# Cross attention rewritten: transposed scores of both heads in row halves, one maximum over a pair's columns, division behind the values

## What is computed

```python
B, N, M = 4, 1024, 77          # batches, queries, keys of the context
H, DH = 16, 64                 # heads; two heads make a pair, so 8 pairs a batch
cross_in = _adaln(x, cond, ...)
ctx_n = _ln(context, ca_lnc_w, ca_lnc_b)
q = _heads(cross_in @ wq); k, v = jnp.split(ctx_n @ wkv, 2, axis=-1)
q, k = _rope(q, sq, cq), _rope(_heads(k), sk, ck)
sim = jnp.einsum('bhnd,bhmd->bhnm', q, k) * DH ** (-0.5)
a = jax.nn.softmax(sim, axis=-1)
o = jnp.einsum('bhnm,bhmd->bhnd', a, _heads(v))
x = o.reshape(...) @ wo + bo + x
```

## Time and profile before

| | us |
|---|---|
| median of 3 runs | 2492.4 (2489.9 to 2494.3) |
| profiled execution | 2491.1 |
| its span in the trace | 2489.3 |
| self attention, from its first load to its last store | 68.5 to 1637.8 |
| cross attention, from its first matmul to the next stage's first load | 1735.9 to 2254.2 |

### The profile page before, as it was taken

One profiled execution on the slowest core, in us unless ns is written; L12 is line 12 of the kernel. 1 busy time (PEld: TensorE's weight loads), 2 busy tenths in 40 slices (PEclk: granted clock), 3 DMA queues, 4 the chain that ended last, 5 costly groups with the idle time before them and its releaser, 6 DMA issues. The chain is left out here.

```text
span 2489.3 us, 40040 instructions
## 1 busy us (share of the span) xinstructions
PE 2229.8 (90%) x15036; PEld 1041.0 (42%) x15036; DVE 1865.8 (75%) x2926; ACT 1330.6 (53%) x1655; POOL 352.3 (14%) x199
## 2 busy tenths in 40 slices
PE   2489999999999999999999999955799999994899
PEld 2133333344333334333334333342456566563566
DVE  6568999986898986898996898665675666665553
ACT  5257676664667664667664666534443434344221
POOL 3100000000000000000000000012653636452100
PEclk9589999999999999999999999976898999996999
DMA  4101101011111010101001100052332323224211
GB/s 163 54 26 40 39 30 41 35 44 43 44 35 44 35 41 30 61 35 44 35 27 44 60 36 20 17 168 54 94 102 72 96 76 93 84 84 128 62 42 34
DMA packets 106254, 143.81 MB, mean 58 GB/s; under 512 B 28209, under 2 KB 74367, under 8 KB 106111
## 3 DMA queue, kind: packets, MB, share of 16 engines
q1 hardware_dynamic: 106111, 141.87, 17.8%
HBM read 55.70 MB, written 12.85 MB: 28 GB/s over the span
## 5 line engine op out<-in xcount | busy, mean ns | idle before, releaser
L625 PE MATMUL sa_ps_o<-sa_probs,sa_v_pair 128*64 128x512 f32 x2048 | 533.5, 615 | 2.9 <-DVE sa_mx L845 2.9
L769 ACT ACTIVATE sa_probs<-sa_ps_s 128x1024 f32<-128x1024 f32 x512 | 495.8, 1025 | 26.2 <-PE sa_ps_s L612 26.2
L845 DVE CUSTOM_DVE_ANT_0 sa_rise<-sa_ps_t,sa_rise 128x512 f32<-128x512 f32 x512 | 333.1, 688 | 200.7 <-PE sa_ps_t L591 200.4
L858 DVE TENSOR_TENSOR sa_acc<-sa_acc,sa_probs 128x1024 f32<-128x1024 f32 x384 | 462.4, 1246 | 7.2 <-ACT sa_probs L769 7.2
L757 ACT ACTIVATE sa_rise<-sa_ps_t 128x1024 f32<-128x1024 f32 x256 | 261.8, 1023 | 258.8 <-PE sa_ps_t L584 258.8
L561 POOL TENSOR_TENSOR sa_xr<-sa_xr,sa_bo_row 128x1024 f32<-128x1024 f32 x8 | 22.6, 2843 | 1322.7 <-DMA sa_xr<-in_x 1322.7
L625 PEld LDWEIGHTS sa_ps_o<-sa_probs,sa_v_pair 128*64 128x64 f32 x2048 | 102.1, 135 | 247.3 <-issue 174.5
L605 PE MATMUL sa_ps_s<-sa_hi 64*128 64x512 f16 x1024 | 194.5, 376 | 0.0
L605 PE MATMUL sa_ps_s<-sa_hi,sa_lo 64*128 64x512 f16 x1024 | 194.4, 376 | 0.0
L605 PE MATMUL sa_ps_s<-sa_lo,sa_hi 64*128 64x512 f16 x1024 | 194.4, 376 | 0.0
L612 PE MATMUL sa_ps_s<-sa_m_line,sa_m_ones 64*128 64x512 f16 x1024 | 189.5, 377 | 1.3 <-DMA sa_m_line<-sa_m_rows 1.3
(11 more groups left out here) (266 smaller groups left out, 4597.5 us busy)
## 6 DMA issues: line engine op xcount, KB each, us to landing
sa_swp<-sa_raw SPq DMA_DIRECT2D x128, 256.0 KB, 2.4
ca_swp<-ca_raw SPq DMA_DIRECT2D x70, 256.0 KB, 2.4
sa_inv<-sa_scratch SPq DMA_DIRECT2D x128, 128.0 KB, 2.9
ca_q_hl<-ca_hi SPq DMA_DIRECT2D x68, 128.0 KB, 2.3
ca_q_hl<-ca_lo SPq DMA_DIRECT2D x68, 128.0 KB, 2.3
sap_xs<-in_x SPq DMA_DIRECT2D x4, 1024.0 KB, 7.0
sa_xr<-in_x SPq DMA_DIRECT2D x4, 1024.0 KB, 5.8
cap_xs<-x_after_self SPq DMA_DIRECT2D x4, 1024.0 KB, 7.0
```

The lines of the kernel that those rows point to most:

```text
L625: ins = pe.matmul(ps_o[rows(x), half(c)], v_pair[:, kt, rows(x)], probs[:, kt % 2, c, half(x)], start=(kt == 0), stop=(kt == NK - 1))
L769: act.activation(probs[:, kt % 2, c, :], ps_s[c][:, :], ACT.Exp, scale=float(DH) ** -0.5).then_inc(s_p, 1)
L845: dve.tensor_tensor_reduce(out=rise[:, half(x)], in0=turn[x], in1=rise[:, half(x)], scale=1.0, scalar=-3.0e38, op0=ALU.add, op1=ALU.max, a ...
L858: dve.tensor_tensor(acc[:, c, :], before, probs[:, kt % 2, c, :], ALU.add).then_inc(s_acc[c], 1)
```

## The change

In `project_context` the upper and lower parts of the keys are written straight into `k_hi` and `k_lo`, both heads of a pair above one another, and the DMAs that stacked them are gone. `cross_attention` is new from its tiles to its order, which is now unrolled:

- The scores are computed twice. `bases` makes the 16-bit product of the upper parts with queries on the partitions, 16 matmuls of 64 rows (8 blocks x 2 heads), only to find a maximum. `maxima` (DVE) takes it over the 77 keys for each query and head, 128 x 16 numbers in one instruction. PE turns them, ACT makes `m_rows` of them (`row`), SP copies these into `m_line` with 4 DMAs (`line`), and PE adds them with `shift`. `scores` makes the three products with the keys on the partitions, for both heads in the two row halves of the array.
- ACT takes the exponentials from PSUM straight into `probs`, keys on the partitions, so the turning of the weights is gone. `values` multiplies at once.
- The sums come from PE (`totals`). ACT brings them to SBUF, SP gathers them (4 DMAs), DVE inverts them, SP writes them to DRAM, waits, and spreads them (4 DMAs). DVE divides the output behind the values (`normalise`, three instructions for each half), three pairs later.
- The rotation is all on DVE (`turned`), and the `q_hl` copies are gone. POOL only adds the bias.
- The output projections of batches 0 to 2 run inside pairs 10, 18 and 26; the last one runs in two parts.

The core of the diff; lines that went with the old stage are left out:

```diff
@@ -983,14 +980,7 @@
                 sp.dma_start(swp[0:P:2, half(n)], raw[1:P:2, half(n)]).then_inc(s_swap[n], 16)
                 sp.dma_start(swp[1:P:2, half(n)], raw[0:P:2, half(n)]).then_inc(s_swap[n], 16)
             for n in range(2):
-                sp.wait_ge(s_hi, n + 1)
-                for x in range(2):
-                    for dst in (k_hh[0:DH], k_hh[DH:P]):
-                        sp.dma_start(dst[:, half(n), x], hi[DH * x:DH * x + DH, half(n)]).then_inc(s_stack, 16)
-                sp.wait_ge(s_lo, n + 1)
-                for x in range(2):
-                    sp.dma_start(k_lo[:, half(n), x], lo[DH * x:DH * x + DH, half(n)]).then_inc(s_stack, 16)
-            sp.wait_ge(s_stack, 16 * 12)
+                sp.wait_ge(s_swap[n], 32)
...
+            def swap(j):
                 sp.wait_ge(s_q_r, 2 * j + 2)
+                if j >= 2:
+                    sp.wait_ge(s_rot, j - 1)
+                sp.dma_start(swp[0:P:2, j % 2, :], raw[1:P:2, j % 2, :]).then_inc(s_swap[j % 2], 16)
+                sp.dma_start(swp[1:P:2, j % 2, :], raw[0:P:2, j % 2, :]).then_inc(s_swap[j % 2], 16)
+            def line(j):
+                sp.wait_ge(s_mt_r, j + 1)
+                for c in range(2):
+                    for x in range(2):
+                        at = TT * c + TT // 2 * x
+                        sp.dma_start(m_line[DH * x:DH * x + 1, half(c)], m_rows[at:at + TT // 2, :]).then_inc(s_line, 16)
+            def gather_sums(g):
+                sp.wait_ge(s_sum_r, g + 1)
+                if g >= 1:
+                    sp.wait_ge(s_scr, 16 * g)
+                for n in range(4):
+                    sp.dma_start(few[32 * n:32 * n + 32, :], sums[32 * n:32 * n + 1, :]).then_inc(s_few, 16)
+            def spread_inverses(g):
+                sp.wait_ge(s_rec, g + 1)
+                if g >= 1:
+                    sp.wait_ge(s_inv, 64 * g)
+                    sp.wait_ge(s_div, 2 * g)
+                sp.dma_start(scratch.rearrange("n (i k) -> (n i) k", k=16), few[:]).then_inc(s_scr, 16)
+                sp.wait_ge(s_scr, 16 * (g + 1))
+                for c in range(2):
+                    for x in range(2):
+                        sp.dma_start(inv[rows(x), half(c)],
+                                     scratch[2 * c + x].partition_broadcast(DH)).then_inc(s_inv, 16)
...
+            for g in range(G + 3):
+                if g == G:
+                    gather_sums(G - 2)
+                if g == G + 1:
+                    gather_sums(G - 1)
+                if 2 <= g < G:
+                    gather_sums(g - 2)
+                if g + 2 < G:
+                    swap(g + 2)
+                if g < G:
+                    line(g)
+                if 2 <= g < G + 2:
+                    spread_inverses(g - 2)
+                if output_batch(g) is not None:
+                    b = output_batch(g)
+                    sp.wait_ge(s_yr, TT * (b + 1))
+                    sp.dma_start(y_v[b], xr[:]).then_inc(s_out, 16)
+                    sp.wait_ge(s_out, 16 * (b + 1))
+                    sp.dma_start(xr[:], x_v[b + 1]).then_inc(s_x, 16)
...
+            def bases(g):
+                b, pair = g // PAIRS, g % PAIRS
                 for t in range(TT):
+                    c, at = t // 4, t % 4 * M
+                    for x in range(2):
+                        ins = pe.matmul(ps_s[:, c, x * HALF + at:x * HALF + at + M],
+                                        hi[rows(x), g % 3, t * P:(t + 1) * P], k_hi[rows(x), pair, b, :],
+                                        start=True, stop=True)
+                ins.then_inc(s_base, 1)
+            def scores(g):
+                b, pair, s = g // PAIRS, g % PAIRS, g % 3
+                for c in range(2):
+                    for n, (k, q) in enumerate(((k_hi, hi), (k_lo, hi), (k_hi, lo))):
+                        for x in range(2):
+                            pe.matmul(ps_s[0:M, c, half(x)], k[rows(x), pair, b, :], q[rows(x), s, half(c)],
+                                      start=(n == 0), stop=False)
+            def shift(g):
+                for c in range(2):
+                    for x in range(2):
+                        ins = pe.matmul(ps_s[0:M, c, half(x)], m_ones[rows(x), 0:M], m_line[rows(x), half(c)],
+                                        start=False, stop=True)
+                    ins.then_inc(s_st, 1)
...
+            def totals(g):
+                for c in range(2):
+                    for x in range(2):
+                        n = 2 * c + x
+                        ins = pe.matmul(turn[0][32 * n:32 * n + 32, :], ones32[0:M, 0:32], probs[:, g % 2, c, half(x)],
+                                        start=True, stop=True)
+                ins.then_inc(s_sum, 1)
...
+            for g in range(G):
+                pe.wait_ge(s_hi, g + 1)
+                if g >= 1:
+                    pe.wait_ge(s_p, 2 * g)
+                bases(g)
+                if g + 3 < G:
+                    if g == 0:
+                        pe.wait_ge(s_q_r, 2 * 2 + 1)
+                    if g >= 2:
+                        pe.wait_ge(s_sum_r, g - 1)
+                    if output_batch(g - 1) is not None:
+                        pe.wait_ge(s_yr, TT * (output_batch(g - 1) + 1))
+                    project(g + 3, 0)
+                pe.wait_ge(s_max, g + 1)
+                pe.wait_ge(s_q_r, 2 * min(g + 3, G))
+                if output_batch(g - 1) is not None:
+                    pe.wait_ge(s_yr, TT * (output_batch(g - 1) + 1))
+                pe.transpose(turn[1][0:2 * TT, 0:P], mx[:, g % 2, :], ident[:, :]).then_inc(s_mt, 1)
+                pe.wait_ge(s_lo, g + 1)
+                scores(g)
+                if g >= 1:
+                    values(g - 1)
+                pe.wait_ge(s_line, 64 * (g + 1))
+                shift(g)
+                if g >= 1:
+                    if g + 3 < G:
+                        pe.wait_ge(s_q_r, 2 * (g + 3) + 1)
+                    elif g >= 2:
+                        pe.wait_ge(s_sum_r, g - 1)
+                    totals(g - 1)
+                if g + 3 < G:
+                    pe.wait_ge(s_mt_r, g + 1)
+                    project(g + 3, 1)
...
+            def evacuate_q(j, c):
+                act.wait_ge(s_q, 2 * j + c + 1)
+                if j >= 2:
+                    act.wait_ge(s_lo, j - 1)
+                act.activation(raw[:, j % 2, half(c)], turn[c], ACT.Copy, scale=1.0 / WS).then_inc(s_q_r, 1)
...
+            def row(g):
+                act.wait_ge(s_mt, g + 1)
+                act.activation(m_rows[:], turn[1][0:2 * TT, 0:P], ACT.Copy, scale=-1.0 / MS).then_inc(s_mt_r, 1)
...
+            for g in range(G):
+                if g + 3 < G:
+                    evacuate_q(g + 3, 0)
+                row(g)
+                if g >= 1:
+                    evacuate_o(g - 1, 0)
+                for c in range(2):
+                    exponentials(g, c)
+                if g >= 1:
+                    evacuate_o(g - 1, 1)
+                    evacuate_sums(g - 1)
+                if g + 3 < G:
+                    evacuate_q(g + 3, 1)
+                if g + 2 < G:
+                    high(g + 2)
+            evacuate_o(G - 1, 0)
+            evacuate_o(G - 1, 1)
...
+            def turned(j):
+                dve.wait_ge(s_swap[j % 2], 32 * (j // 2 + 1))
+                dve.tensor_tensor(raw[:, j % 2, :], raw[:, j % 2, :], ropeC[:, :], ALU.mult).then_inc(s_mul, 1)
+                dve.tensor_tensor(swp[:, j % 2, :], swp[:, j % 2, :], ropeS[:, :], ALU.mult).then_inc(s_mul, 1)
+                dve.wait_ge(s_mul, 2 * (j + 1))
+                dve.tensor_tensor(raw[:, j % 2, :], raw[:, j % 2, :], swp[:, j % 2, :], ALU.add).then_inc(s_rot, 1)
+            def low(j):
                 dve.wait_ge(s_hi, j + 1)
+                dve.tensor_tensor(lo[:, j % 3, :], raw[:, j % 2, :], hi[:, j % 3, :], ALU.subtract).then_inc(s_lo, 1)
+            def maxima(g):
+                dve.wait_ge(s_base, g + 1)
+                banks = ps_s.rearrange("p c (x n) -> p (c x) n", x=2)[:, :, 0:4 * M]
+                dve.reduce_max(mx[:, g % 2, :], banks.rearrange("p a (t m) -> p a t m", m=M), AX_X).then_inc(s_max, 1)
+            def reciprocals(g):
+                dve.wait_ge(s_few, 64 * (g + 1))
+                dve.reciprocal(few[:], few[:]).then_inc(s_rec, 1)
+            def normalise(g, c):
+                n, cs = 2 * g + c + 1, half(c)
+                dve.wait_ge(s_inv, 64 * (g + 1))
+                dve.wait_ge(s_oev, n)
+                dve.tensor_tensor(o_pair[:, g % 2, cs], o_pair[:, g % 2, cs], inv[:, cs], ALU.mult).then_inc(s_div, 1)
+                dve.wait_ge(s_div, n)
+                dve.tensor_copy(o_hi[:, g % PAIRS, cs], o_pair[:, g % 2, cs]).then_inc(s_ohi, 1)
+                dve.wait_ge(s_ohi, n)
+                dve.tensor_tensor(o_lo[:, g % PAIRS, cs], o_pair[:, g % 2, cs], o_hi[:, g % PAIRS, cs],
+                                  ALU.subtract).then_inc(s_ot, 1)
...
```

(85 more changed lines are left out.)

373 lines of the change are left out of this document (114 added, 259 removed).

## The result

| | before | after |
|---|---|---|
| median, us | 2493.4 (2489.9 to 2498.6, 4 runs) | 2597.8 (2596.9 to 2600.9, 4 runs) |
| span of the profiled execution, us | 2489.3 | 2599.1 |
| PE busy in the span | 90% | 85% |

The profiled execution took 2600.9 us, where the prediction had 2602.

What follows compares the result with a forecast made beforehand. PE bounds the old kernel; in the new one the chain through DVE, ACT, SP and PE does. Stage 55 + 445 + 66 + 22 + 48 = 636 us against 518.3, less 6.5 for its earlier start: 2603 us, range 2545 to 2655.

Steps and rivals of the forecast that it cites:

- the chain: One pair's waits through PE, DVE, ACT and SP: 12.4 us before the last step, 17.1 with it, against 12.0 before.
- Row and line: From ACT's start on the row to the first matmul on the line, with four SP DMAs: 4.2 us.
- The last step: PE's shift, totals and half a projection: 2.95 us at the upper clock, 5.4 after idling; taken as 4.7.
- Two lists: Work per pair on two queues: SP issuing 15 DMAs, 9.6 us; DVE's instructions, 10.3 us; both staying behind the chain.
- Rival 1: PE's clock holds in the last step: pair 15.4 us, stage 591, kernel 2558 us; chance 0.22.
- three output projections: Output projections inside pairs lie open, since DVE and ACT run through their lists and wait: 3 x 22 = 66 us.
- pairs 29 and 30: Late pairs where no evacuation stands ahead of the row: 11 us each, 22 us.
- end: After the last maxima: outputs of pairs 29 to 31 divided in turn, then last projection part and store: 48 us.
- SP's delay behind an output: After each output projection SP waits for the store, gathers and swaps before the line: about 1 us late.
- Rival 2: Narrow matmuls are slow and keep the clock down: bases 2.2 us, pair 19.4, kernel about 2663 us; chance 0.13.
- Rival 3: The chain isn't closed; ACT goes straight to the row: pair 10.5 us, kernel 2431, deciding point 12.8; chance 0.07.
- Rival 4: Row halves don't run side by side with 77 key columns: shift 0.43 us more per pair, kernel 2614 us; chance 0.03.

Runs made afterwards that it cites:

- low_first: Changed kernel with one edit on DVE: low(g+1) directly behind maxima(g), ahead of normalise(g-3). 2495.8 us.
- row_first: Changed kernel with one edit on ACT: the row of maxima of pair g ahead of the query copy for pair g+3. 2482.6 us.
- fill: Changed kernel with the scores of each pair computed three times more, where PE waits for the line. 2564.5 us.
- line2: Changed kernel with the line of maxima copied by two DMAs of eight rows instead of four. 2563.7 us.
- row_low_line: Changed kernel with row ahead of the copy on ACT, low(g+1) ahead of normalise(g-3) on DVE, and the line in two DMAs. 2456.9 us.
- row_low_line_fill: row_low_line with the scores of each pair computed once more than needed, behind the values. 2443.7 us.
- fill4: Changed kernel with the scores of each pair computed four times more, where PE waits for the line. 2563.8 us.

## Why the prediction was right, point by point

**The bound and the chain.** PE does not set the pair; the chain over DVE, ACT and SP does. PE's own work fell from 81.78 us in seven pairs, 11.7 each at a granted clock of 0.93, to 8.4 at 1.00 (the first row of `low_first` above), and the pair still grew. `low_first` and `row_first` each break it at one link and give back 102 and 115 us, where the whole loss was 104. Here the pair by its steps, predicted and measured in the timeline above:

| step | predicted | measured |
|---|---|---|
| first of `bases` to DVE's start on `maxima` | 1.25 | 0.75 |
| `maxima` | 1.43 | 1.44 |
| to the start of `low` (division of g-3) | 3.65 | 3.49 |
| `low`, to ACT's start on the copy | 1.25 | 1.31 |
| copy | 0.65 | 0.49 |
| row, line, to `shift` (1877.52 to 1881.44) | 4.2 | 3.92 |
| `shift`, `totals`, projection | 4.7 | 5.54 |
| pair | 17.1 | 16.94 |

The mechanism is right. Three terms were mis-sized, and that they cancelled to within 0.2 us was luck. `bases` were put 0.5 us too long: the 64-row matmuls that alternate between row halves take 0.70 us for 16, 0.044 each, below both bounds of the prediction (0.056 and 0.14). Row and line were put 0.3 us too long. The last step was put 0.8 us too short: taken at 4.7 between 2.95 and 5.4, it is 5.54 in the trace, above the upper end that the earlier trace rows gave. That end had the clock come back after 4.9 us. Here all matmuls of the step ran at the lower clock, and the first at the upper one (0.38 us) starts at 1888.82, 7.4 us behind the shift. Two lists were put too long without a part in the sum: SP issues for 9.0 us a pair, not 9.6, and DVE has 9.7 us and not 10.3. DVE's 9.7 became the bound of the short pairs above. That DVE doesn't wait for the inverses holds at 17 us, but no longer at 14.

**The clock.** The prediction took the lower clock for most of the step because of an idle time of 6.2 us; it was 5.42. The page "TensorE: Matmul & The Clock Gate" of the Trainium skill, section "HAM oscillation — how this bites in real kernels", has a loop that waits for a DMA in every tile start each one cold. With that the trace agrees: the seven pairs ahead of the first output projection stand at a granted clock of 0.70 and last 16.9 to 17.0 us. Rival 1, the upper clock throughout, is what `fill` brought about in part, with a last step of 2.95 us and pairs of 14.1.

**The line.** The prediction added 1.4 us to the 2.8 of two DMAs. It was 1.1: 2.78 in `line2`, 3.92 here. What it gave for two DMAs less, 36 us, `line2` measured at 34; 26 x 1.14 are 30 of them, the rest came from the clock.

**The stage.** In us:

| part | predicted | measured |
|---|---|---|
| start, to `bases` of pair 3 | 55 | 54.5 |
| 26 pairs | 445 | 440.4 |
| three output projections | 66 | 70.4 |
| pairs 29 and 30 | 22 | 19.4 |
| end | 48 | 49.3 |
| stage | 636 | 634.0 |
| stage begins at | 1729.4 | 1730.8 |

The 26 pairs are 26 x 16.94; what the stretch from pair 3 to pair 29 has above that (2296.84 - 1786.06 = 510.8) is the outputs', 23.5 each. The term for SP's delay behind an output was too small: 21.3 to 21.7 us pass in the pair itself (38.68 - 16.94 in two of the three), and the pair behind it is 1.0 to 3.2 us longer than others, not 1. The last two pairs are 9.7 us and not 11; the shorter `bases` and line are 0.8 of that. At the end the inverses of one pair after the other each took their way through DRAM, with DVE idle:

```profile
2330.37 0.69 DVE L1419 TENSOR_TENSOR ca_o_pair<-ca_o_pair,ca_inv 128x512 f32<-128x512 f32 x1 [6.18 <-DMA ca_inv<-ca_scratch]
...
2340.42 0.69 DVE L1419 TENSOR_TENSOR ca_o_pair<-ca_o_pair,ca_inv 128x512 f32<-128x512 f32 x1 [6.21 <-DMA ca_inv<-ca_scratch]
```

10.05 us apart, against 10.1.

**The rivals.** Rival 2 falls: narrow matmuls are fast, though its last step of 5.9 us was nearer to 5.54 than the 4.7 of the forecast. Rival 3, a faster kernel through a chain that isn't closed, didn't come about in this order, but it is what `row_low_line` and `row_low_line_fill` made of it: below a mean pair of about 12.5 us (`low_first`, level with the kernel before) the new stage wins, near the 12.8 that the prediction gave as the point. Rival 4 falls: four `shift` matmuls take 0.63 us in `fill`. One takes 0.38 and the next of the same kind starts 0.22 behind it, so four in a row would need about 1.0, two pairs side by side 0.60: the row halves do run side by side with 77 columns.

What stays open: what decides in which pairs the clock falls. 12 matmuls more took the pairs at the lower clock from 7 of 20 to 2 (`fill`, `fill4`), so the idle time that is left has a part in it, but pairs of the same work still differ.

## What to carry to other kernels

Before a rewrite that saves work on the bounding engine, follow one iteration through every in-order queue: here 6.6 us of matrix work a pair was taken away, half of it put back in other forms, and 4.7 us of wait was put ahead of the one small instruction on which everything stood. An instruction for the present iteration should stand ahead of those for earlier and later ones; two lines moved gave back 119 us. When the matrix engine's idle time returns in each iteration, look at its clock in the rows behind the gap, and add that loss to the gap.
